# Adjacency visits in fewer, longer runs inside the mixing and first-layer products of a graph kernel

## What is computed

```python
xn = _layernorm(x, axis=-1)
# gnn_layer: h = x @ W.T + b ; agg = segment_sum(h[src], dst) ; relu(agg)
# mix: q = softmax(x @ Wq.T, -1) * dim**-0.5 ; k = softmax(x @ Wk.T, -2)
#      context = k^T v ; x = q @ context + x ; x @ W1.T @ W2.T + x
x = x + _L0_gnn_ref(xn, edge_index, W1, b1, W2, b2) + _L0_mix_ref(xn[None], Wq, Wk, Wv, W1, W2)[0]
x = x + _L0_ffn_ref(_layernorm(x, axis=-1)[None], gate_weight, experts)[0]
```

## Time and profile before

| | us |
|---|---|
| median of 3 executions | 466.75 (466.54 to 467.08) |
| the profiled execution | 466.17 |
| its span in the profile | 464.4 |
| PE busy in it | 449.4 (97%) |
| DVE busy in it | 321.1 (69%) |
| ACT busy in it | 150.0 (32%) |
| granted TensorE clock, mean share of full | 0.998 |

### The profile page before, as it was taken

How to read it: one execution, slowest core, us unless ns; L and a number is a source line. 1 busy time by engine, 2 the same in 40 slices (tenths; PEclk the granted TensorE clock), 3 DMA queues, 4 the chain that set the end, 5 groups by cost and what they waited for, 6 DMA issues and landing times.

```text
span 464.4 us, 6828 instructions
## 1 busy us (share of the span) xinstructions
PE 449.4 (97%) x2411; PEld 359.5 (77%) x2411; DVE 321.1 (69%) x1103; ACT 150.0 (32%) x273; POOL 62.8 (14%) x91
## 2 busy tenths in 40 slices
PE   8999999999999999999999999999999998888995
PEld 5777788887888888887779999877777776655883
DVE  4888699879988988888972110444645666777972
ACT  4666575304223223341223110322133114551110
POOL 4415700000000000000004000002300000006642
PEclk9999999999999999999999999999999999999999
DMA  8920200390000000003000000002744449305891
GB/s 254 271 72 1 92 0 1 95 218 22 2 1 1 1 1 1 0 3 99 28 1 4 1 1 1 1 0 59 276 134 134 132 140 378 145 1 182 310 349 70
DMA packets 20414, 40.44 MB, mean 87 GB/s; under 512 B 2521, under 2 KB 2851, under 8 KB 20373
## 3 DMA queue, kind: packets, MB, share of 16 engines
q1 hardware_dynamic: 18117, 32.53, 22.8%
q0 software_dynamic: 2256, 7.39, 4.4%
HBM read 30.09 MB, written 10.31 MB: 87 GB/s over the span
## 4 chain that ended last, share of the span: by engine, by line
PE 86%; DVE 9%; ACT 3%; issue 1%; POOLq 0%; DVEq 0%
PE ps L742 40%; PE ps L1058 9%; PE ps L980 9%; PE ps L867 6%; PE ps L729 4%; PE ps L921 2%; PE ps L784 2%; PE ps L1194 2%; ACT scrap_a L1460 1%; PE ps L1075 1%; PE ps L1164 1%; PE ps L1007 1%; PE ps L897 1%; PE ps L765 1%; PE ps L1035 1%
## 5 line engine op out<-in xcount | busy, mean ns | idle before, releaser
L1755 DVE TENSOR_SCALAR RING_D<-places,PLACES 125x170 bf16<-125x170 f16 x260 | 70.6, 272 | 0.0
L1756 DVE TENSOR_SCALAR RING_S<-iota,HOME 125x128 bf16<-125x128 f16 x260 | 67.2, 259 | 0.0
L980 PE MATMUL ps<-AT,H1H 125*128 125x416 f32 (+1 forms) x108 | 38.0, 352 | 0.2 <-issue 0.2
L980 PE MATMUL ps<-AT,H1L 125*128 125x416 f32 (+1 forms) x108 | 38.0, 351 | 0.0
L729 PEld LDWEIGHTS ps<-RING_D,RING_S 125*125 125x125 bf16 x260 | 28.7, 136 | 10.0 <-DVE RING_S L1756 0.4
L1058 PE MATMUL ps<-H2H,AT 125*125 125x512 f32 x90 | 36.1, 402 | 0.0
L1058 PE MATMUL ps<-H2L,AT 125*125 125x512 f32 x90 | 35.5, 394 | 0.0
L1075 PE MATMUL ps<-WE0H 128*128 128x512 f32 x129 | 35.4, 408 | 0.0
L1898 DVE SCALAR_TENSOR_TENSOR ZL<-ps,ZH 128x416 fp32r<-128x416 f32 (+1 forms) x12 | 6.3, 585 | 39.1 <-ACT ZH L1402 39.1
L729 PE MATMUL ps<-RING_D,RING_S 125*125 125x170 bf16 x260 | 32.4, 237 | 0.2
L609 POOL TENSOR_TENSOR G2L<-RAW_G,G2H 128x512 fp32r<-128x512 f32 x4 | 5.0, 1301 | 189.0 <-ACT G2H L1213 189.0
(11 more groups left out here) (411 smaller groups left out, 1159.1 us busy)
## 6 DMA issues: line engine op xcount, KB each, us to landing
RAW_E<-in_experts SPq DMA_DIRECT2D x8, 1024.0 KB, 9.9
RAW_AGAIN<-in_experts SPq DMA_DIRECT2D x3, 1024.0 KB
X<-in_x SPq DMA_DIRECT2D x1, 2240.0 KB
out_x<-X SPq DMA_DIRECT2D x10, 224.0 KB
scratch<-X SPq DMA_DIRECT2D x10, 224.0 KB
scratch<-Y SPq DMA_DIRECT2D x10, 224.0 KB
RAW_A<-in_mW SPq DMA_DIRECT2D x4, 256.0 KB, 4.3
RAW<-in_mW2T SPq DMA_DIRECT2D x4, 256.0 KB, 5.3
```

Source lines behind the costliest of these rows:

```text
L980: pe.matmul(place(f), h[0:TT, k, 128 * f:128 * (f + 1)], AT[0:TT, k, c0:c1], start=(k == 0 and n == 0), stop=False)
L1755: V.tensor_scalar(hot_d(v, width(b)), places[0:ET, 0:width(b)], PLACES[0:ET, c:c + 1], None, ALU.is_equal)
L1756: V.tensor_scalar(hot_s(v), iota[0:ET, :], HOME[0:ET, c:c + 1], None, ALU.is_equal).then_inc(done["marked"], 1)
```

## The change

Three things change.

PE's places are taken apart from DVE's chunks. DVE still marks chunks of three or four visits, but `visits_in_products(True)` merges what stands before products 0 and 6 of a unit (and 12 and 18) into one run, placed at the later of the two, 6 (or 18). This holds for x0 to x9, q2 to q9 and h0 to h8. `cp`, q0 and q1 keep their places. A mixing tile has then three runs of seven or eight visits where it had six of three or four, and a first-layer tile one run of six where it had one of two and one of three. In all PE has 48 runs where it had 86. The visits, 291, stay the same.

Seven visits move on to the first layer: the four at place 6 of q1 and the three at place 12 of x9 are gone, and the places 0 of h0 to h8 hold three instead of two. All visits between shift by four or seven.

DVE's order is changed at both ends of the mixing loop. At the start the chunk of q1 is marked before the last two of the four `context_left`, `q_peak(0)` stands before the last of them, and no chunk stands between `q_peak(0)` and `q_inverse(0)`. At the end (i = NT) `q_left(9)` comes first, ahead of `add_mix(8)` and of any chunk.

```diff
--- before.py
+++ after.py
@@ -188,17 +188,25 @@
 ORDER = [(b, s) for b in range(NB) for s in range(VISITS[b])]
 
 
-def visits_in_products():
+def visits_in_products(long):
 
 
     spots = [("cp", n, 3) for n in range(0, 48, 6)]
     for i in range(NT + 1):
         if i < NT:
-            spots += [(f"q{i}", 0, 4), (f"q{i}", 6, 4 if i % 4 == 1 else 3)]
+            spots += [(f"q{i}", 0, 4)]
+            if i != 1:
+                spots += [(f"q{i}", 6, 4 if i % 4 == 1 else 3)]
         if i:
-            spots += [(f"x{i - 1}", n, 3 if n == 12 else 4) for n in (0, 6, 12, 18)]
+            spots += [(f"x{i - 1}", n, 3 if n == 12 else 4) for n in (0, 6, 12, 18) if (i, n) != (NT, 12)]
     for i in range(NT - 1):
-        spots += [(f"h{i}", 0, 2), (f"h{i}", 6, 3)]
+        spots += [(f"h{i}", 0, 3), (f"h{i}", 6, 3)]
+    if long:
+        runs = {}
+        for unit, n, count in spots:
+            later = unit[0] in "xh" or unit[0] == "q" and int(unit[1:]) > 1
+            runs[unit, 12 * (n // 12) + 6 if later else n] = runs.get((unit, 12 * (n // 12) + 6 if later else n), 0) + count
+        spots = [(unit, n, count) for (unit, n), count in runs.items()]
     found, v = [], 0
     for unit, n, count in spots:
         count = min(count, NV - v)
@@ -209,8 +217,8 @@
     return found
 
 
-CHUNKS_OF_VISITS = visits_in_products()
-VISITS_AT = {(unit, n): vs for unit, n, vs in CHUNKS_OF_VISITS}
+CHUNKS_OF_VISITS = visits_in_products(False)
+VISITS_AT = {(unit, n): vs for unit, n, vs in visits_in_products(True)}
 IN_A = VISITS_AT["q0", 6][-1] + 1
 
 
@@ -1785,29 +1793,28 @@
             context_left(0)
             context_left(1)
             mark_next()
+            mark_next()
             context_left(2)
+            q_peak(0)
             context_left(3)
-            mark_next()
-            for i in range(NT + 1):
-                if i < NT and i:
+            q_inverse(0)
+            for i in range(1, NT + 1):
+                if i < NT:
                     mark_next()
+                else:
+                    q_left(i - 1)
                 if i >= 2:
                     add_mix(i - 2)
-                if i < NT and i:
-                    mark_next()
+                mark_next()
                 if i < NT:
                     q_peak(i)
-                if i == 0:
-                    mark_next()
-                if i:
                     mark_next()
                     q_left(i - 1)
-                    mark_next()
+                mark_next()
                 if i < NT:
                     q_inverse(i)
-                if i:
                     mark_next()
-                    mark_next()
+                mark_next()
                 if i == NT - 1:
                     for c in range(C):
                         split_lo("g1", c)
@@ -1829,7 +1836,7 @@
             dve.wait_ge(loads["b1"], 16)
             for i in range(NT):
                 if marked[0] < len(CHUNKS_OF_VISITS):
-                    mark_next(2)
+                    mark_next(min(2, len(CHUNKS_OF_VISITS) - marked[0]))
                 add_bias(1, i)
                 if i:
                     h1_left(i - 1)
```

## The result

| | before | after |
|---|---|---|
| median, us (6 executions each, side by side) | 466.64 (466.49 to 467.08) | 464.0 (463.79 to 464.37) |
| the profiled execution | 466.17 | 463.92 |
| its span | 464.4 | 462.2 |
| PE busy | 449.4 | 447.8 |
| DVE busy | 321.1 | 321.1 |

The ratio is 0.9946, with a 95% interval from 0.9936 to 0.9956: 2.5 us less (2.1 to 3.0). The forecast was 463.95 us.

The account below looks back on a forecast made before the run. PE was taken to bound the kernel, with DVE next and PE waiting for it at both ends. Runs 1.41, first stall 0.82 and last stall 0.57 sum to 2.80 us: 466.75 - 2.80 = 463.95 us, range 463.3 to 465.4.

Parts of the forecast that it names:

- The price of a run: On PE's path, each run costs a fixed 0.037 us; 38 fewer give 1.4 us (0.95 to 1.9).
- The first stall: In q1, PE's waits for DVE's marked visits, 0.55 and 0.27 us, both go: 0.82 us.
- The walk that asked what is late next: After q1, PE wants QTL at 116.7 and can go on at 116.5 to 116.6: slack 0.1 to 0.2 us.
- The last stall: In x9, PE's wait for QTL goes as QTL comes directly behind G1L: 0.57 us, with 0.7 to spare.
- The steady tiles: In the middle mixing tiles, DVE's work stays 9.35 us, tiles get about 0.1 us shorter, no new stall: 0.
- The first layer: Seven more visits there cost PE 0; its tile takes 3.28 us, DVE's 3.2: full, but it fits.
- The bound of 0.7 us: First layer: upper bound on cost, 0.08 us per tile in nine, if DVE is slower by a few hundredths a visit.
- Loads that set the pace: Rival: in runs over four visits, weight loads set the pace, 470.7 us at 0.137 each; slower, by loads or DVE, 0.08.
- DVE taking part back: Rival: DVE loses 0.3 us at the first QTL and 0.7 in the first layer, 464.95 us; with mildly slower loads 0.18.
- the stall moving to x0: Rival: q1's stall only moves to x0's run of eight or its QTL; 0.82 not won, 464.8 us, within the 0.18.
- No change and slower: Whole time: no change, 466.7 us with loads at about 0.10 us, chance 0.05; slower, by loads or DVE-bound stage, 0.08.
- 10 visits on, at least 1.4 us away: Steady tiles: the group needing ACT's copied bank starts ten visits on, at least a 1.4 us gap away: cost 0.

Follow-up runs that it names:

- e5: Changed kernel with one run of 15 visits per x unit at place 18 and a ring of 27; 464.91 us, ratio 0.9967.
- e7: Changed kernel with only the sum into X put back ahead of QTL of tile 9, no marked visits; 463.37 us, one execution.
- e4: Changed kernel with DVE's old order at the end: sum into X and four visits before QTL of tile 9; 464.79 us, ratio 0.9957.
- e11: Changed kernel with seven visits in h0, h1 and h2 and none in h8; 464.3 us, ratio 0.9955.
- e1: Kernel before with only PE's runs merged, no visit moved, DVE's order old; 465.58 us, ratio 0.9976.
- e3: Changed kernel with DVE's old order at the start of the mixing stage; 464.48 us, ratio 0.995.
- e2: Changed kernel with the short runs put back, 83 instead of 48; moved visits and new DVE order stay; 465.16 us, ratio 0.9967.
- e9: Changed kernel with a ring of 27 and runs of 15 in x units except x0, x5 and x7; 464.09 us, ratio 0.9942.
- e12: Changed kernel with ring of 27, runs of 15 except in x0, x5, x7, x9, x9's three visits back, h8 empty; 463.4 us, ratio 0.9937.
- e10: Changed kernel with x9's three visits back and none in h8, DVE's new order kept; 463.54 us, ratio 0.9935.
- e6: Changed kernel with each visit over half its columns, 85 instead of 170, weight loads unchanged; 460.69 us, one execution.

## Why the prediction was right, point by point

**The total and its sign**: 463.95 forecast, 464.0 measured, and 2.54 us in the middle where the sum had 2.80. Nearly all of the 0.26 us too much is one term, the price of a run. The medians stand 2.64 apart, and the forecast started from 466.75, where before measured 466.64 beside the changed kernel. So the closeness of 463.95 and 464.0 is in part luck, of a tenth or two.

**The price of a run: right in kind, mis-sized.** The sum had 38 x 0.037 = 1.41 us. Both experiments on it give 0.031 by the middles, so 38 x 0.031 = 1.18; this lies inside the stated 0.025 to 0.05. The step that was off is the arithmetic with hundredths. With the starts taken in ns, a visit follows a visit by 76, the first product follows the last visit by 28, the second product the first by 314, and otherwise a product the one before by 233; the visit after a product follows it by 229. A run costs then 28 + 314 + 229 - 76 - 2 x 233 = 29 ns beyond its visits. The middles gave 31, since the gap before AT's products is in them; of the 2.54 us about 1.10 are the runs, 1.37 the stalls and 0.06 that gap. The pattern isn't tied to bf16: behind the four turns, which are f32, the first product follows by 29 ns and the second by 314 too (after, 113.43 and 113.74 us). The forecast had a visit at 0.075, which over four visits puts 4 ns too much into the price, and did not see that the product ahead of a run is 4 ns short. The long run shows it in the plain timeline: eight visits in 0.87 and 15 in 1.40 us give 0.076 a visit.

**The first stall: right, 0.82 forecast.** The starts in ns give 0.55 and 0.27. With the start undone 0.50 came back (a stall of 0.53), and the second stall stayed away with its run. The walk that asked what is late next came out as well: the forecast had PE at QTL's place at 116.7 and QTL started by 115.8. In after, 0.29 us later in the clock of the span, they stand at 116.91 and 116.06. PE went on 0.73 us after QTL's start in rows 7 and 8, so 116.79 here: a slack of 0.12 us, as forecast (0.1 to 0.2). e5, which took the run of eight away from ahead of it (0.64 us), stalled there by 0.58: a slack of 0.06.

**The last stall: right, 0.57 forecast.** By the starts in ns it was 0.56, and after has none. The room was larger than forecast: 206.71 + 0.73 = 207.44 against PE at 208.67 is 1.23 us instead of 0.7. G1L waited 0.52 us for ACT's G1H before and doesn't after, and I had left that wait in. e7 agrees: the sum of 0.6 us ahead of QTL was harmless. e4 agrees on the other side: the sum and four visits, 0.6 + 1.34 us, exceed 1.23 by 0.7, and the stall was 0.80.

**The steady tiles: right.** 10.55 us by the windows (10.5 forecast), no wait of PE on DVE's marks, and DVE still waits 1.0 us before each maximum.

**The first layer: right at 0, and as full as feared.** DVE's timeline, the bias of two tiles in a row:

```profile
228.39 0.70 DVE L1826 TENSOR_TENSOR ps<-ps,bias 125x512 f32<-125x512 f32 x1
...
231.27 0.26 DVE L1763 TENSOR_SCALAR RING_D<-places,PLACES 125x170 bf16<-125x170 f16 x1
231.45 0.25 DVE L1764 TENSOR_SCALAR RING_S<-iota,HOME 125x128 bf16<-125x128 f16 x1
231.65 0.70 DVE L1826 TENSOR_TENSOR ps<-ps,bias 125x512 f32<-125x512 f32 x1
```

From one bias to the next it is 3.26 us here and 3.27 in the mean of the tiles with six visits, and PE's tiles take 3.27 too (forecast 3.28). DVE's one-hot comparisons follow each other by 0.16 to 0.18 us, but the bias, which needs PE's products of the tile, comes 0.20 us behind the last of them. So DVE keeps PE's pace and waits some 0.03 us a tile, too short to be listed as a wait. Its own work is 3.23 us, as forecast (3.2), and those 0.03 are all that it has to spare. PE did not wait. The bound of 0.7 us was not touched, though with one more visit per tile DVE's 3.57 us would be longer than PE's 3.35 (an estimate from these spacings; no kernel here has it in the whole layer).

**The rivals.** Loads that set the pace: refuted, by the run of eight, the run of 15 and the half columns. DVE taking part back and the stall moving to x0: not seen in after, though a slack of 0.1 us was all that kept the second away, and e5 shows what it looks like. No change and slower: out, as the interval ends at 0.9956.

**What the prediction didn't have.** The gap before AT's products holds PE up by 0.38 us in before and by 0.32 in after. The wait for "issue" there was in the profile before (the rows don't show it; the product at 246.37 above does). It was not a cost of the change, whose gain even has those 0.06 us in it, but it was worth a third of a microsecond to whoever put the last group earlier. And the longer runs have a limit the prediction put at "10 visits on, at least 1.4 us away": the bank of the group after next. In after that held, in e5 and e11 it did not.

## What to carry to other kernels

Price a change of kind between matmuls from the starts, as a fixed amount per run, and check it with the longest run, where rounding counts least; merging runs is then worth its count times that price at most. Before moving work away from ahead of an operand that another engine makes late, walk to the next such operand: what stood there was its cover. The new or longer stalls here (e1 and e5 at QTL, e5 and e11 at a bank) are where PE came too soon, and in e3 and e4 DVE's part came too late. A gap put down to "issue" ahead of a product can still go with a late operand; moving its producer up is the test.

## What the runs showed of the hardware

- A run of bf16 visits between fp32r products of 512 columns costs about 0.029 us of PE's time beyond its visits by the starts, for runs from two to eight (0.031 by the middles of e1 and e2, with the gap before AT's products in them). Where the merged run has 15, each run saved brought less: 0.18 / 7 = 0.025 (e9), 0.24 / 10 = 0.024 (e5), 0.11 / 6 = 0.019 (e12 against e10). Why it is less is open.
- The weight load of 125 columns is recorded at 0.137 us, yet visits follow each other every 0.058 us where the matmul has 85 columns (e6) and every 0.076 us where it has 170 (after). The recorded duration of a load is no bound on the pace.
- Behind the last matmul of a short kind, visits of 170 columns in bf16 as well as the f32 turns, a product of 512 columns starts after 0.028 us, and the next one 0.314 us later, where products in a row are 0.233 us apart (after).
- The first product with AT started 0.55 us behind its predecessor when its operand's copy began 1.69 us before (after). When the copy began 4.17 us before, it followed by 0.23 (e10, e11). Where between the two it turns was not measured.
